# Causal masking of the diagonal tiles: GpSimd selects in place of half of TensorE's mask products

## The reference

```python
x = x + 0.5 * ffn(layernorm(x), ...)
x = x + attention(layernorm(x), w_qkv, w_proj)
x = x + 0.5 * ffn(layernorm(x), ...)

# attention, 16 heads of 8 numbers each, N = 1024
att = jnp.einsum('bhnd,bhmd->bhnm', q, k) * scale
att = att + slopes[None, :, None, None] * jnp.arange(N)[None, None, None, :]
att = jnp.where(causal, att, big_neg)        # causal = tril(ones(N, N))
att = jax.nn.softmax(att, axis=-1)
out = jnp.einsum('bhnm,bhmd->bhnd', att, v)
```

## Time and profile before

| | |
|---|---|
| median of 3 runs | 1014.22 us (1011.94 to 1020.28) |
| the profiled execution | 1006.91 us, its span 1005.0 us |
| PE | 915.0 us busy, 91% |
| PEld | 566.9 us, 56% |
| DVE | 659.6 us, 66% |
| ACT | 509.7 us, 51% |
| POOL | 386.5 us, 38% |
| L1925, the mask products of the second pass | 512 instructions, 219 ns median each |
| chain that ended last | PE 53%, DMA 19%, DVE 11%, issue 6%, POOL 5% |

### The profile page before, as it was taken

The page is one execution under the profiler, slowest core; times in us unless marked ns, Lnnn a source line. Parts: engine busy times, 40 slices in busy tenths (PEclk is TensorE's granted clock), DMA queues, the critical chain, the costliest instruction groups (busy, mean ns, idle before and its releaser), DMA issues.

```text
span 1005.0 us, 19516 instructions
## 1 busy us (share of the span) xinstructions
PE 915.0 (91%) x6961; PEld 566.9 (56%) x6961; DVE 659.6 (66%) x1697; ACT 509.7 (51%) x826; POOL 386.5 (38%) x447
## 2 busy tenths in 40 slices
PE   5798979888897999999999999999999888969996
PEld 4576979762443444544444445444453347969864
DVE  5856325558695688797788877887868547324422
ACT  2333646440264566556655565665556654636531
POOL 4375655463671500002201005007500465564564
PEclk9979989995798999999999999999999997979998
DMA  9712545355102231400423102304000013546432
GB/s 300 229 48 76 175 125 166 98 165 139 47 4 51 70 87 28 97 4 17 117 51 74 26 1 86 87 13 96 4 3 1 27 48 103 171 120 163 129 84 66
DMA packets 84260, 85.36 MB, mean 85 GB/s; under 512 B 11732, under 2 KB 73444, under 8 KB 81700
## 3 DMA queue, kind: packets, MB, share of 16 engines
q1 hardware_dynamic: 50842, 55.08, 20.6%
q0 software_dynamic: 8192, 16.79, 6.0%
q10 hardware_dynamic: 25132, 12.26, 4.1%
HBM read 52.48 MB, written 37.45 MB: 89 GB/s over the span
## 4 chain that ended last, share of the span: by engine, by line
PE 53%; DMA 19%; DVE 11%; issue 6%; POOL 5%; ACT 2%; DVEq 2%; POOLq 1%; SPq 0%
PE banks L1939 10%; PE banks L1909 9%; DMA region_c<-sorted_y,pos 9%; PE banks L1922 9%; PE banks L1831 6%; PE banks L1843 6%; DMA region_b<-sorted_y,pos 4%; DVE nmax L1493 3%; DMA sorted_x<-region_b,pos 2%; POOL sorted_x L824 2%; PE banks L1925 2%; PE banks L1912 2%; PE banks L1819 2%; PE banks L1703 1%; DVE nmax_late_keys L1493 1%
## 5 line engine op out<-in xcount | busy, mean ns | idle before, releaser
L1077 ACT ACTIVATE work<-banks 128x1024 f32<-128x1024 f32 (+3 forms) x384 | 300.4, 812 | 234.3 <-PE banks L1925 185.5
L1493 DVE TENSOR_REDUCE nmax<-banks 128x1 f32<-128x512 f32 (+3 forms) x432 | 271.7, 665 | 49.8 <-PE banks L1909 23.5
L1909 PE MATMUL banks<-ks,qs 75*128 75x512 bf16 (+3 forms) x576 | 183.3, 347 | 10.4 <-DVE nmax L1493 5.8
L824 POOL DMA_INDIRECT sorted_x<-region_b,pos x112 | 113.3, 1012 | 142.0 <-DVEq L1315 76.7
L1939 PE MATMUL banks<-work,vaug 128*9 128x512 f32 (+3 forms) x1536 | 161.3, 492 | 0.0
L1922 PE MATMUL banks<-qs,ks 78*128 78x512 bf16 (+3 forms) x576 | 154.3, 330 | 4.1 <-ACT work L1077 3.2
L1373 DVE COPY region_c<-w 128x512 f32 x184 | 73.2, 439 | 110.5 <-PE banks L1843 101.1
L1493 DVE TENSOR_REDUCE nmax_late_keys<-banks 128x1 f32<-128x384 f32 (+3 forms) x176 | 109.4, 638 | 43.2 <-PE banks L1912 38.5
L1909 PEld LDWEIGHTS banks<-ks,qs 75*128 75x128 bf16 x576 | 55.9, 99 | 136.4 <-DVE nmax L1493 71.5
L1831 PE MATMUL banks<-xTp,region_c 128*128 128x128 f32 x736 | 102.4, 284 | 3.0 <-ACT xTp L977 2.5
L1925 PE MATMUL banks<-identb,maskb 128*128 128x128 bf16 x512 | 103.3, 221 | 0.0
(11 more groups left out here) (212 smaller groups left out, 1172.5 us busy)
## 6 DMA issues: line engine op xcount, KB each, us to landing
xld<-sorted_x SPq DMA_DIRECT2D x92, 128.0 KB
sorted_y<-ysb ACTq DMA_DIRECT2D x92, 128.0 KB
qs<-q_scr SPq DMA_DIRECT2D x36, 192.0 KB
ks<-k_scr SPq DMA_DIRECT2D x36, 192.0 KB
q_scr<-qp SPq DMA_DIRECT2D x15, 256.0 KB
region_c<-q_scr SPq DMA_DIRECT2D x12, 192.0 KB
region_c<-k_scr SPq DMA_DIRECT2D x12, 192.0 KB
k_scr<-kp SPq DMA_DIRECT2D x9, 256.0 KB
```

Of the source, the lines that this page charges most:

```text
L824: nc.gpsimd.indirect_dma_start(out=sorted_x[r], out_offset=bass.IndirectOffsetOnAxis(ap=pos[r][:, k, t:t + 1], axis=0), in_=xh_tile(f, r * ...
L1077: nc.scalar.activation(pT[s % 2][pair][:, :, 0:w], ps_s[pair][:, :, 0:w], ACT.Exp).then_inc(s_e, 1)
L1493: nc.vector.tensor_reduce(dst, ps_in_turn[SLOT["bank", u * NB + n]][:, 0:len(pieces) * w].rearrange("p (h j) -> p h j", j=w), axis=AXX, op ...
L1909: last = mm(dst, qs[g][0:PASS1_ROWS, h, it * P:(it + 1) * P], ks[g][0:PASS1_ROWS, h, j0:j0 + w], start=True, stop=not diagonal)
```

## The change

In 64 of the 128 diagonal steps the mask products are dropped. In place of them GpSimd sets the exponentials above the diagonal to zero after ScalarE has written them, with one `affine_select` for each pair of heads (two heads by 128 columns, fp32), and `weigh` of that step waits for it. These are all 8 diagonal steps of the units (0,3), (1,0), (1,3), (2,0), (2,3), (3,2), and the steps from 8 on of (0,2), (1,2), (2,2), (3,1).

So that unmasked scores stay small where they are largest, eight contraction rows are added to the second pass (86 in place of 78). Row c is 1 for the first 64 queries of tile c and -1e30 for the last 64 keys of tile c, so the products with it mask a quarter of each diagonal tile. GpSimd builds these rows once in a tile `corners` (8 partitions, 2x8x128 bf16), ahead of the first gather. The SP queue copies them to the first three groups' `qs` and `ks` with six DMAs, and later to those of g = 3 with two.

GpSimd's loop over the batches is unrolled, with its work placed between the selects. Among other moves, the copy of the last value tile now stands behind the select of the next batch's first step.

```diff
+ALL_ROWS = PASS2_ROWS + BT
...
+SELECTS = [(b, g, s) for b in range(BATCH) for g in range(UNITS) for s, (jt, i0, _, _) in enumerate(STEPS)
+           if i0 == jt * P and ((b, g) in ((0, 3), (1, 0), (1, 3), (2, 0), (2, 3), (3, 2))
+                                or (b, g) in ((0, 2), (1, 2), (2, 2), (3, 1)) and s >= AHEAD)]
...
+def selected(b, g, s):
+    return 2 * (SELECTS.index((b, g, s)) + 1)
...
+            def corner_rows():
+
+                sp.wait_ge(s_cor, 1)
+                for g in range(UNITS - 1):
+                    for i, rows in enumerate((qs[g][PASS2_ROWS:ALL_ROWS], ks[g][PASS2_ROWS:ALL_ROWS])):
+                        sp.dma_start(rows, corners[:, i, :, :].rearrange("p c n -> p (c n)").unsqueeze(
+                            1).to_broadcast([BT, GH, SEQ])).then_inc(s_corl, 16)
...
             for g in range(1, UNITS - 1):
                 load_rows(g)
+            corner_rows()
             max_rows(0, 0)
...
+            sp.wait_ge(s_corl, 16 * 2 * (UNITS - 1))
+            for rows in (qs, ks):
+                sp.dma_start(rows[UNITS - 1][PASS2_ROWS:ALL_ROWS], rows[0][PASS2_ROWS:ALL_ROWS, :, :]
+                             ).then_inc(s_alr, 16)
...
+            def select(b, g, s):
+
+                for pair in range(2):
+                    pool.wait_ge(s_e, 2 + (b * UNITS + g) * 2 * NS + 2 * s + pair + 1)
+                    probs = pT[s % 2][pair][:, :, 0:P]
+                    nc.gpsimd.affine_select(out=probs, in_=probs, compare_op=ALU.is_ge, fill=0.0, base=0,
+                                            pattern=[[0, 2], [1, P]], channel_multiplier=-1).then_inc(s_sel, 1)
...
+            nc.gpsimd.memset(corners[:, :, :, :], 0.0)
+            pool.drain()
+            nc.gpsimd.memset(corners[:, 0, :, 0:P // 2], 1.0)
+            nc.gpsimd.memset(corners[:, 1, :, P // 2:P], MASKED)
+            pool.drain()
+            for i in range(2):
+                nc.gpsimd.affine_select(out=corners[:, i, :, :], in_=corners[:, i, :, :], compare_op=ALU.is_equal,
+                                        fill=0.0, base=0, pattern=[[-1, BT], [0, P]], channel_multiplier=1)
+            pool.drain().then_inc(s_cor, 1)
             gather(0, 0, 0, GATHER_FIRST)
...
-            with pool.Fori(0, BATCH - 1) as b:
-                norm(b + 1)
-                make_parts(b + 1, len(START) + b * len(USES), USES)
-                pool.wait_ge(s_free, 2 + len(START) + b * len(USES) + [u[3] for u in USES].index("v1"))
-                values(b + 1)
+            for b in range(BATCH - 1):
+                base = len(START) + b * len(USES)
+                for g in range(UNITS):
+                    for s in range(NS):
+                        if (b, g, s) in SELECTS:
+                            select(b, g, s)
+                        if b and (g, s) == (0, 0):
+                            value(b, BT - 1)
+                        if (g, s) == (1, 0):
+                            norm(b + 1)
+                        if (g, s) == (1, 7):
+                            make_queries(b + 1, base, USES)
+                        if (g, s) == (1, NS - 1):
+                            make_keys(b + 1, base, USES)
+                        if (g, s) == (2, NS - 1):
+                            pool.wait_ge(s_free, 2 + base + [u[3] for u in USES].index("v1"))
+                        if g == UNITS - 1 and s >= NS - BT + 1:
+                            value(b + 1, s - (NS - BT + 1))
+            value(BATCH - 1, BT - 1)
 
             ffn_norms(1, range(BATCH - 1))
+            for b, g, s in SELECTS:
+                if b == BATCH - 1:
+                    select(b, g, s)
...
                 jt, i0, w, ih = STEPS[s]
+                masked = i0 == jt * P and (b, g, s) not in SELECTS
...
-                              qs[g][:, h, i0:i0 + w], start=True, stop=not diagonal)
-                    if diagonal:
+                              qs[g][:, h, i0:i0 + w], start=True, stop=not masked)
+                    if masked:
                         last = mm(ps_s[pair][:, j, 0:P], maskb[:, :], identb[:, :], start=False, stop=True)
...
                 pe.wait_ge(s_e, 2 + u * 2 * NS + 2 * s + 2)
+                if (b, g, s) in SELECTS:
+                    pe.wait_ge(s_sel, selected(b, g, s))
```

More of the change, by code:

```diff
@@ L295, in build @@
         one = sb("one", [P, 1])
+        corners = sb("corners", [BT, 2, BT, P], BF16)
         stats = sb("stats", [P, GT, 6])
@@ L407, in build @@
         late_rows = region_c[:, :, :].rearrange("p a n -> p (a n)").bitcast(BF16).rearrange(
-            "p (a h n) -> p a h n", a=2, h=GH)[0:PASS2_ROWS]
-        qs = [sb(f"qs{g}", [PASS2_ROWS, GH, SEQ], BF16) for g in range(UNITS - 1)] + [late_rows[:, 0]]
-        ks = [sb(f"ks{g}", [PASS2_ROWS, GH, SEQ], BF16) for g in range(UNITS - 1)] + [late_rows[:, 1]]
+            "p (a h n) -> p a h n", a=2, h=GH)[0:ALL_ROWS]
+        qs = [sb(f"qs{g}", [ALL_ROWS, GH, SEQ], BF16) for g in range(UNITS - 1)] + [late_rows[:, 0]]
+        ks = [sb(f"ks{g}", [ALL_ROWS, GH, SEQ], BF16) for g in range(UNITS - 1)] + [late_rows[:, 1]]
         ONES_ROWS = 16 * 2 * (UNITS - 1)
@@ L517, in build @@
         s_ones = sem("a_ones_loaded")
+        s_cor = sem("a_corners_made")
+        s_corl = sem("a_corners_loaded")
         s_alw = sem("a_bias_written")
@@ L529, in build @@
         s_e = sem("a_probs")
+        s_sel = sem("a_probs_selected")
         s_pv = sem("a_outputs")
@@ L856, in values, with value @@
             def values(b):
+                for jt in range(BT):
+                    value(b, jt)
+            def value(b, jt):
                 v = vst[:, :, :].rearrange("p t (h d) -> p t h d", d=DH)
-                for jt in range(BT):
-                    if not isinstance(b, int):
-                        pool.wait_ge(s_pv, 2 + b * UNITS * NS - (BT - 1 - jt))
-                    nc.gpsimd.tensor_tensor(vaug[:, jt, :, 0:DH], v[:, jt, :, :],
-                                            one[:, :].unsqueeze(2).to_broadcast([P, HEADS, DH]),
-                                            ALU.mult).then_inc(s_va, 1)
+                if b:
+                    pool.wait_ge(s_pv, 2 + b * UNITS * NS - (BT - 1 - jt))
+                nc.gpsimd.tensor_tensor(vaug[:, jt, :, 0:DH], v[:, jt, :, :],
+                                        one[:, :].unsqueeze(2).to_broadcast([P, HEADS, DH]),
+                                        ALU.mult).then_inc(s_va, 1)
+            def select(b, g, s):
[4 more added lines that the diff above has]
+                                            pattern=[[0, 2], [1, P]], channel_multiplier=-1).then_inc(s_sel, 1)
             def norm(b):
@@ L877, in make_parts, with make_keys @@
                 pool.drain().then_inc(s_parts, 1)
+            def make_keys(b, base, names):
+                at = {n: i for i, (_, _, _, n) in enumerate(names)}
                 pool.wait_ge(s_free, base + at["k1"] + 2)
@@ L1913, in first_pass, with scores @@
                 last.then_inc(s_b1, 1)
-            def scores(u, g, s, pair):
+            def scores(u, b, g, s, pair):
                 jt, i0, w, ih = STEPS[s]
+                masked = i0 == jt * P and (b, g, s) not in SELECTS
                 pe.wait_ge(s_e, u * 2 * NS + 2 * s + pair + 1)
@@ L2016, in steps @@
                                 pe.wait_ge(s_mrow, 16 * (u1 + 1))
-                            scores(u1, g1, s1, int(what[1]))
+                            scores(u1, u1 // UNITS, g1, s1, int(what[1]))
                         elif what == "w":
@@ L2051, in _ @@
             pe.wait_ge(ffn[0].u, RING + NH * CHUNKS + ROUTED)
-            scores(0, 0, 0, 0)
-            scores(0, 0, 0, 1)
+            pe.wait_ge(s_corl, 16 * 2 * (UNITS - 1))
+            scores(0, 0, 0, 0, 0)
+            scores(0, 0, 0, 0, 1)
             steps(0, FIRST_STEPS, [])
```

5 lines of the change are left out of this document (2 added, 3 removed).

## The result

| | before | changed |
|---|---|---|
| median of 4 runs each, on one chip | 1013.08 us (1010.29 to 1020.28) | 1027.57 us (1020.93 to 1030.86) |
| ratio, with its 95% interval | | 1.0119 [1.008, 1.0158] |
| the profiled execution, its span, mean clock | 1006.91, 1005.0, 0.950 | 1020.93, 1019.0, 0.934 |
| PE / DVE / ACT / POOL busy, us | 915.0 / 659.6 / 509.7 / 386.5 | 916.4 / 659.5 / 508.4 / 441.1 |

Forecast were 1004.0 us and a range that ended at 1011. The sign was wrong.

The account below looks back on a forecast made before the run. The PE was taken to bound the attention, VectorE next. The terms -15.0 + 0.3 + 0.5 + 1.1 + 1.5 + 0.9 + 0.5 made -10.2 us, from 1014.2 to 1004.0 us, range 997.5 to 1011.

Parts of the forecast that it names:

- GpSimd's new work ahead of the attention: Building `corners` before the first gather, 5.5 to 8.1 us of work, would cost 0.5 us, 0 to 8.
- At no cost: six more DMAs: On SP's queue, behind the loads of g = 2, the added DMAs would cost nothing while it waits for the first maxima.
- The PE's turn: In the attention, removing 256 mask products of 0.0586 us each would gain 15.0 us gross, less losses at later waits.
- The maxima's waits: DMA waits for the maxima's rows would lose 0.47 us each at (1,2) and (2,3), 0.2 in (0,2): 1.1 us.
- The select: Each GpSimd select would take 0.45 us and fit narrowly before the weighing in step 0; stray waits 0.3 us in all.
- the rival "slower": Selects much slower than their row would hold up steps 0 and 9 to 11: about 1030 us, chance 0.06.
- Who holds up whom: VectorE instructions reading two SBUF tensors could delay a select, by 0.15 us in step 0; below 1.7 us by the skill's rule.
- 86 rows at zero: Score products with 86 contraction rows would cost nothing extra; upper end 0.8 us.
- Rival 2: Gain mostly given back, by the build shifting gathers 4 us or more or by later waits: 1008 to 1011, chance 0.27.

Follow-up runs that it names:

- e3: The changed kernel with only the build of `corners` moved early, the six DMAs left in place: 1013.16 us, ratio 1.0019 to the kernel before.
- e2: The changed kernel with both the build of `corners` and the six DMAs moved early: 1014.44 us, ratio 1.0024 to the kernel before.
- e4: As e2, but without selects and with every mask product kept on TensorE: 1014.0 us, ratio 1.0001 to the kernel before.
- e10: The changed kernel with the build early, the six DMAs in place, no selects and all mask products: 1017.85 us, ratio 1.0056 to the kernel before.
- e1: The changed kernel without selects, all mask products kept, corner rows and DMAs at the change's places: 1023.15 us, ratio 1.0114 to the kernel before.
- e11: As e4, plus the 128 selects working from a constant tile to an unread tile, no weighing waiting: 1015.61 us, ratio 1.0038 to the kernel before.
- e7: As e2, with all selects and their waits, but every mask product kept too: 1019.07 us, ratio 1.0068 to the kernel before.
- e8: As e2, with neither selects nor mask products in the 64 steps, so masking is partly left out: 1004.77 us, ratio 0.9918 to the kernel before.
- e5: The kernel before without the drain ahead of the first gather: 1015.87 us, ratio 1.0043 to the kernel before.

## Why the prediction was wrong

- **The failing step: "GpSimd's new work ahead of the attention", 0.5 us taken.** I named both readings, 0 "if the idle time is a true wait for the stores, up to 8 if it is a fixed cost that the build adds to", and took the first, on no row that showed the gather waiting for a store; the row said `<-issue`, that is for nothing visible. It is a fixed cost. The build itself took 5.2 us, near my lower estimate of 5.5, and moved the first gather by 5.3. The ladder prices it at 5.4 ± 2.9 us without selects.
- **"At no cost: six more DMAs".** I looked at SP's queue alone, where they indeed hold up nothing. They move their data while GpSimd's gathers are paced by landing DMAs, and these lead to the PE's stall. Price 4.5 ± 1.8 us without selects; between e3 and e2 the time doesn't show it. The stall of 5.70 us was in my rows: what delays the gathers delays the end of this stall (the first gather comes 5.3 us later, gather 44 12.9, the stall's end 13.7). My mark for it, "no longer than 6.5 us", failed with 13.99.
- **The PE's turn: right in sum, in part by luck.** 15.0 gross less 0.3, 0.5, 1.1, 1.5 and 0.9 makes 10.7 us; the part at full clock shrank by 9.7 ± 1.7, and e3's attention, where the clock held, by 9.4. My mark was that (0,3), (1,3) and (2,3) get some 1.7 us shorter: they got 0.6, 1.3 and 2.1 shorter in the changed kernel, and 1.6, 1.5 and 2.1 in e2, where the clock held in them. The maxima's waits came out otherwise than forecast. I expected them at the ends of (1,2) and (2,3), 0.8 us and more: there the changed kernel has none, and even the two of before (0.34 and 0.91 us) are gone. Before (0,3), where I had put 0.2 us, it waits 1.56. Why the two went isn't shown.
- **A term that was missing: the clock.** I took the clock of 1.00 as given because it had been 1.00. With selects in place of products it fell for stretches, and 6 to 12 us went there. Step by step from the kernel before to the changed one, in mean span: +0.8 ± 2.0 (86 rows, prepared early: e4), +4.5 (DMAs in place: e10), +5.4 (late build: e1), and +3.1 ± 6.6 (selects for products, -9.1 of work and +12.2 of clock) make +13.9 ± 6.7. The steps must add up to that, since each starts where the last ended; it is their sizes that the runs show.
- **The select: right** in duration (0.41) and fit (no weighing waits in step 0); the rival "slower" named the select and so had the right sign for the wrong reason. (Its price for a select of 1.5 us is also added up wrongly: by its own room it would be 40 us, not 28.) The select's real cost is small: +1.3 ± 2.2 us by being there (e11 - e4), +3.3 ± 2.8 more where it writes the exponentials and the weighing waits (e7 - e11). In the traces' attention it is 1.0 us in e11 and 2.4 in e7 against e4, and falls almost wholly on the last steps of (0,2), (1,2) and (2,3), where the next scores wait for the maxima's rows: in e7 0.94, 0.63 and 0.57 us. These waits scatter by as much without any select (0.31 to 1.33 us behind (1,2) in e4, e10 and e1).
- **Who holds up whom: mostly the other way round.** I feared that VectorE would hold up a select. The 128 selects of the changed kernel took 406 to 418 ns each; VectorE's instructions with two SBUF inputs took longer beside them (the last section has the rows). In e7 eight selects took 479 to 626 ns where such an instruction of VectorE's met them.
- **86 rows at zero: right.** Score products have the same mean, 330 ns, and the kernel with the rows and nothing else stands at 1.0001.
- Rival 2 had the mechanism of the build (gathers shifted by 4 us or more onto the stall), at 0.27; its end, 1011, assumed one loss, not three together.

**What stays open.** Why the clock falls there. The runs show when (products gone and selects present), not by what. The engine's busy share before the fall doesn't tell e2 from e8 at 750 us. Waits of the PE stand before other falls (1.56 and 1.25 us in the changed kernel, 1.25 at 788.5 us in e2), but they are not enough by themselves: the wait of 1.65 us before (0,3) in e2, and those of 1.25 us at both places in e3, left the clock at 1.00. Whether a fall comes differs between executions of one kernel, and each kernel has one trace. The Trainium skill tells of an oscillating clock where the PE pauses briefly and often between groups of matmuls (TensorE: Matmul & The Clock Gate, "A second HAM failure mode: psum-queue depth-cycling"); the 0.02 us of pauses in seven speak against it for the fall at 750.9. I tried no kernel that fills the freed turns with other PE work while the selects stay at half number.

## What to carry to other kernels

An idle time that ends with `issue` must not be filled in thought: put new work there only after a row shows what the engine waits for; an idle time that ends with another engine's name (the 16.09 us before the first scatter) can take it. Small DMAs that cost their queue nothing can still delay an engine that is paced by landing DMAs, so follow the stall of the bound engine back to its source and keep new transfers out of that stretch. When PE work is thinned out, compare the mean granted clock over all runs as well as the time: a saving of 1% of the work was given back here by 0.01 of clock.

## What the runs showed of the hardware

- The first drain on GpSimd behind its indirect DMAs takes some 5 us more than it otherwise would: 5.36 us of idle time before `corners` is filled, and 6.87 in place of 1.63, 5.2 more, for a later one when the first was left out (e5). Even 9.29 us of waiting for VectorE in between did not absorb it, so it doesn't look like time that the DMAs need to finish. The Trainium skill says that the first call of code newly loaded on GpSimd pays about 6 us in which the profile shows no instruction (GPSIMD Engine Reference, "2.1 Instruction dispatch"). Size, the missing instruction and the way it passed whole to the next drain agree with that; no run here shows the load itself.
- An `affine_select` of 256 fp32 elements took 406 ns against 294 for 128: 0.87 ns an element beyond a fixed 0.18 us. One of 1024 bf16 on 8 partitions took 1.09 us, against 1.08 by these two figures. The Trainium skill prices data-dependent branching on GpSimd at about 12 cycles an element (GPSIMD Engine Reference, "Elementwise — side-by-side cycle accounting"); that would be 10 ns an element by my estimate at 1.2 GHz, and the measurement, 0.87 ns, decides against it for this select.
- VectorE's combining of the maxima (L1568, two SBUF inputs) takes 0.17 us alone. Where it started 0.10 us after a select, at 549.14 and 683.01 us in the changed kernel, it took 0.34, and 1.07 where it started 1.09 us into a GpSimd product of 2.14 us. Each time it ended 0.03 us after GpSimd's instruction. The selects took their 406 to 407 ns. In the timelines of POOL and DVE:

```profile
549.04 0.41 POOL L902 TENSOR_SCALAR_AFFINE_SELECT work<-work 128x256 f32<-128x256 f32 x1 [0.51 <-ACT work L1145]
549.14 0.34 DVE L1568 TENSOR_TENSOR nmax<-nmax,nmax_late_keys 128x16 f32<-128x16 f32 x1
...
581.88 0.17 DVE L1568 TENSOR_TENSOR nmax<-nmax,nmax_late_keys 128x16 f32<-128x16 f32 x1
```
- The PE's granted clock fell from 1.00 to 0.50 within a microsecond, at 750.9 us in e2, though the engine had idled 0.02 us in the seven before, and stayed there for 13 us. A falling clock need not have a long wait ahead of it.
